# The feed-forward part of a Mamba block: channels on the partitions, ternary first weights, steps between the drain's slots

## The reference

```python
x = x + attn(layernorm(x))            # Mamba: 32 heads of 64, state 64, 8 groups
x = x + ffn(layernorm(x))

def layer_norm(x, g, b):              # biased variance, eps 1e-5
    return (x - mu) * rsqrt(var + eps) * g + b
def ternary_quant(w):
    scale = 1.0 / clip(mean(abs(w)), 1e-5)
    wq = clip(round(w * scale), -1.0, 1.0) / scale
    return w + stop_gradient(wq - w)  # in value: wq
def ffn(x):
    h = layer_norm(x, ln1_g, ln1_b)               # 128 features
    h = h @ ternary_quant(w1).T + b1              # to 512
    h = gelu(h, approximate=False)
    h = layer_norm(h, ln2_g, ln2_b)               # over 512
    return h @ ternary_quant(w2).T + b2           # to 128
```

## Time and profile before

| what | us |
|---|---|
| runs shown | 1182.76, 1175.94, 1181.65 (median 1181.65) |
| the profiled execution | 1176.72 |
| its span, first to last instruction | 1174.8 |
| busy in the span: PE, DVE, ACT, POOL | 1052.5 (90%), 1092.0 (93%), 969.3 (83%), 859.4 (73%) |

### The profile page before, as it was taken

The page is one execution under the profiler, slowest core; times in us unless marked ns, Lnnn a source line. Parts: engine busy times, 40 slices in busy tenths (PEclk is TensorE's granted clock), DMA queues, the critical chain, the costliest instruction groups (busy, mean ns, idle before and its releaser), DMA issues.

```text
span 1174.8 us, 26568 instructions
## 1 busy us (share of the span) xinstructions
PE 1052.5 (90%) x8966; PEld 734.7 (63%) x8966; DVE 1092.0 (93%) x2040; ACT 969.3 (83%) x2832; POOL 859.4 (73%) x596
## 2 busy tenths in 40 slices
PE   1724789999999999999999999999999999976886
PEld 1613566766766676776676667676666766643665
DVE  7597999999999999999999999999999999757985
ACT  2766989999999999999999999999999999823543
POOL 7300368888888888888888888888888888993331
PEclk9998999999999999999999999999999999989999
DMA  7310000000000000000000000000000000103001
GB/s 166 126 72 0 11 2 1 1 2 2 28 2 2 1 28 1 2 2 28 1 2 1 28 2 2 2 28 1 2 1 20 2 2 2 37 30 117 29 25 37
DMA packets 28756, 24.94 MB, mean 21 GB/s; under 512 B 12112, under 2 KB 22992, under 8 KB 28368
## 3 DMA queue, kind: packets, MB, share of 16 engines
q1 hardware_dynamic: 21584, 21.16, 5.9%
q10 hardware_dynamic: 7040, 2.12, 0.7%
HBM read 14.88 MB, written 8.39 MB: 20 GB/s over the span
## 4 chain that ended last, share of the span: by engine, by line
PE 73%; DVE 14%; issue 6%; POOL 3%; ACT 2%; ACTq 1%; POOLq 0%; DVEq 0%
PE bank L1596 10%; PE bank L1578 9%; PE bank L1610 8%; PE bank L1511 8%; PE bank L1527 8%; PE bank L1513 6%; PE bank L1512 6%; PE bank L1567 5%; PE bank L1548 5%; DVE conv L1127 4%; PE bank L1649 3%; PE bank L1621 2%; DVE lm L1117 2%; PE bank L1441 1%; PE bank L1662 1%
## 5 line engine op out<-in xcount | busy, mean ns | idle before, releaser
L1127 DVE SCALAR_TENSOR_TENSOR conv<-bank,cw,conv 128x509 f32<-128x509 f32 (+2 forms) x576 | 420.2, 740 | 16.0 <-ACT conv L725 8.6
L621 POOL TENSOR_TENSOR lm<-lm,cbs 128x1024 f32<-128x1024 f32 x128 | 304.1, 2376 | 69.3 <-ACT xw L820 69.3
L1117 DVE TENSOR_TENSOR_SCAN lm<-bank,ident 128x512 f32<-128x512 f32 x256 | 298.5, 1207 | 1.0 <-PE bank L1527 1.0
L865 ACT ACTIVATE xdt<-bank,dt_all 128x64 f32<-128x64 f32 x1024 | 221.5, 327 | 35.4 <-PE bank L1548 35.4
L820 ACT ACTIVATE xw<-xdt,lm 128x64 f32<-128x64 f32 x768 | 198.9, 363 | 0.0
L629 POOL TENSOR_TENSOR ssum<-ssum,sq 128x512 f32<-128x512 f32 x96 | 123.1, 1283 | 89.4 <-ACT sq L880 88.9
L1511 PE MATMUL bank<-xn_hi,w_hi 128*128 128x512 f32 x320 | 164.6, 514 | 15.1 <-DVE conv L1127 14.3
L602 POOL TENSOR_TENSOR gated<-gated,gate 128x512 f32<-128x512 f32 x128 | 164.6, 1286 | 15.0 <-DVE gated L1174 13.2
L611 POOL TENSOR_TENSOR gated<-gated,rbs 128x512 f32<-128x512 f32 x128 | 165.3, 1292 | 1.1 <-ACT rbs L949 1.1
L831 ACT ACTIVATE conv<-bank,cb_bias,cw 128x512 f32<-128x512 f32 x189 | 141.2, 779 | 11.0 <-PE bank L1513 6.5
L1596 PEld LDWEIGHTS bank<-lm,xdt 128*64 128x64 f32 x2048 | 109.9, 137 | 63.4 <-issue 63.4
(11 more groups left out here) (175 smaller groups left out, 1780.4 us busy)
## 6 DMA issues: line engine op xcount, KB each, us to landing
lm<-in_L_attn_in_proj_w SPq DMA_DIRECT2D x1, 2048.0 KB, 11.6
xn_scratch<-chan SPq DMA_DIRECT2D x4, 512.0 KB, 4.7
r_stage<-residual_scratch SPq DMA_DIRECT2D x8, 256.0 KB, 2.9
x_scratch<-r_stage SPq DMA_DIRECT2D x8, 256.0 KB, 2.0
cbs<-x_scratch SPq DMA_DIRECT2D x8, 256.0 KB, 2.9
gated<-x_scratch SPq DMA_DIRECT2D x1, 2048.0 KB, 7.9
out_tokens<-gated ACTq DMA_DIRECT2D x8, 256.0 KB, 2.3
xn_stage<-xn_scratch SPq DMA_DIRECT2D x7, 256.0 KB, 3.2
```

The source lines that it names most:

```text
L621: gp.tensor_tensor(lm[:, mr, :, :], lm[:, mr, :, :], cbs[:, :, :], ALU.mult).then_inc(m_done, 1)
L865: act.activation(xdt[:, r, at:at + HP], misc_of("xt", n)[:, at:at + HP], ACT.Copy, scale=dt_h).then_inc(xdt_done, 1)
L1117: V.tensor_tensor_scan(lm[:, m % R, a, :], bc_bank[(3 * m + a) % 2][:, :], ident4[:, :], 0.0, ALU.mult, ALU.add).then_inc(scanned, 1)
L1127: V.scalar_tensor_tensor(out=conv[:, ci % 4, shift:S], in0=tile_bank(b, n, t)[:, 0:S - shift], scalar=cw[:, q, t, KW - 1 - shift:KW - shif ...
```

## The change

`step(i)` is rewritten for all engines, and its channels now lie on the partitions throughout. The normalised rows (without scale) are transposed as before; ACT writes them times g1 as float32r (`high_rows`), DVE the rest (`low_rows`). w1 becomes a matrix of -1, 0 and 1 (`w1q`, float32r), so that the first product is two single-piece products of 512 columns for each of four tiles, into two banks in turn. Its scale and bias (b1 and the part that comes from b of the norm, `b1s`) are operands of the Gelu. The hidden layer norm is moved behind the second product: w2 times g2 is centred over its rows and scaled (`centre_second`), a column pair with 1/sqrt(512) gives the sums of the hidden channels (WCOL = 130 columns), ACT squares the hidden tiles, DVE and POOL add the four of them, PE sums them over partitions (`square_sums`), DVE forms the variance (`hidden_variance`), POOL the power (`hidden_root`), and DVE multiplies and adds onto the rows (`results`). b2 and the part of b of the norm become one row `bias2`, which POOL adds to the rows (`add_bias`).

The steps stand behind slots of the drain, by engine, and all quantising behind its slots 0 to 5. In the drain norm products of m >= LATE_M = 8 are made by DVE instead of POOL. Each batch's rows have a place of their own (`fx[i]`, in tensors as they fall free); batch 7's stay where they are made. SP stores the results. The loop over steps is written out. The core of the diff (removed `step` and `quantise` bodies stand in the listing above; other bodies are cut to their waits and work):

```diff
-SUM_SLOTS, QUANT_SLOTS, QUANT_END = (5, 6), (6, 7), 12
-EARLY_STEPS = {12: -2, 13: -1, 14: 0}
+LATE_M = SLOTS - 8
+PE_STEPS = {4: (0,), 6: (1,), 8: (2,), 10: (3,), 14: (4,), 15: (5, 6, 7, 8)}
+ACT_STEPS = {4: (0,), 7: (1,), 8: (2,), 13: (3,), 14: (4,), 15: (5, 6, 7)}
+DVE_STEPS = {4: (0,), 6: (1,), 8: (2,), 13: (3,), 14: (4,), 15: (5, 6, 7, 8, 9)}
+POOL_STEPS = {4: (0,), 7: (1,), 8: (2,), 13: (3,), 14: (4,), 15: (5, 6, 7, 8, 9)}
...
+            sp.wait_ge(cdec_done, NB * SLOTS - R)
+            sp.wait_ge(skipped, NB * SLOTS - 7)
+            load(0)
+            load(1)
...
+            sp.wait_ge(xdt_done, 2 * CH * NB * SLOTS)
+            load(2)
+            load(3)
             sp.wait_ge(m_done, NB * SLOTS)
+            load(4)
+            load(5)
...
+            for i in range(NB):
+                sp.wait_ge(f_out, CH * i + CH)
+                sp.dma_start(out[i].rearrange("(c p) d -> p c d", p=P), fx[i]).then_inc(f_stored, 16)
...
@@ gpsimd @@
                     bb, m = back(b, n, LAG_NORM)
+                    if b == NB and m >= LATE_M:
+                        return
...
+            def row_root(i):
+                gp.wait_ge(f_xaggr, CH * i + CH)
+                gp.tensor_tensor(ve_x, mv_x[:, :, 1], eps_c[:, 0:CH], ALU.add).then_inc(f_xeps, 1)
+                gp.tensor_tensor(r_x, ve_x, neghalf[:, 0:CH], ALU.pow).then_inc(f_xr, 1)
+            def hidden_root(i):
+                gp.wait_ge(f_y, 2 * i + 2)
+                gp.tensor_tensor(r_h, ve_h, neghalf[:, 0:CH], ALU.pow).then_inc(f_hr, 1)
+            def add_bias(i):
+                gp.wait_ge(q_bias2, 1)
+                gp.tensor_tensor(fx[i], fx[i], bias2..., ALU.add).then_inc(f_xb, 1)
+            def add_squares(i):
+                gp.wait_ge(f_add_v, i + 1)
+                for t in range(2, HT):
+                    gp.wait_ge(f_sq, HT * i + t + 1)
+                    gp.tensor_tensor(total, total, fsq[t][0], ALU.add).then_inc(f_add, 1)
+            def step(i):
+                hidden_root(i - 2)
+                add_bias(i - 1)
+                row_root(i + 2)
+                add_squares(i)
...
+                if n == 1:
+                    row_root(0)
+                if n == 3:
+                    row_root(1)
...
@@ scalar @@
+            def gelu(i, t):
+                act.wait_ge(f_mm1, HT * i + t + 1)
+                act.activation(fge[:, i % 2, t, :], h_bank[t % 2][:, :], ACT.Gelu, scale=qs[:, 12:13],
+                               bias=b1s[:, t:t + 1]).then_inc(f_gelu, 1)
+            def step(i):
+                gelu(i, 0)
+                gelu(i, 1)
+                high_rows(i + 1)
+                hidden_square(i, 0)
+                gelu(i, 2)
+                hidden_square(i, 1)
+                gelu(i, 3)
+                if i == 2:
+                    expand_root(NB, 9)
+                hidden_square(i, 2)
+                hidden_square(i, 3)
...
+                if n == 1:
+                    act.wait_ge(q_load, 32)
+                    for k in range(2):
+                        act.activation(qt[:, k, :], qw[:, k, :], ACT.Abs, accum_out=qs[:, k:k + 1]).then_inc(q_abs, 1)
+                if n == 3:
+                    act.wait_ge(q_t, 1)
+                    act.activation(w1q[:, :], bank[2][:, :], ACT.Copy).then_inc(q_copied, 1)
+                    high_rows(0)
+                    for k in range(2):
+                        act.wait_ge(q_rows, k + 1)
+                        act.activation(qw[:, 0, :], (qw[:, 1, :], qt[:, 1, :])[k], ACT.Copy, accum_out=qs[:, 16 + k:17 + k]).then_inc(q_acc, 1)
+                        act.wait_ge(q_acc, k + 1)
+                if n == 4:
+                    act.wait_ge(q_t, 2)
+                    act.activation(w2x[:, :, 0:DM], bank[3]..., ACT.Copy).then_inc(q_copied, 1)
...
@@ vector @@
+                if b == NB and n >= LATE_M + LAG_NORM - SLOTS and back(b, n, LAG_NORM) is not None:
+                    V.tensor_tensor(gated[:, v % 2, m % R, :], gated[:, v % 2, m % R, :], rbs[:, :], ALU.mult).then_inc(normed_v, 1)
...
+            def results(i):
+                dve.wait_ge(f_hr, i + 1)
+                dve.wait_ge(f_xb, i + 1)
+                for c in range(CH):
+                    V.scalar_tensor_tensor(out=fx[i][:, c, :], in0=result_bank..., scalar=r_h[:, c:c + 1],
+                                           in1=fx[i][:, c, :], op0=ALU.mult, op1=ALU.add).then_inc(f_out, 1)
+            def step(i):
+                hidden_variance(i - 2)
+                row_stats(i + 2)
+                results(i - 2)
+                low_rows(i + 1)
+                row_normalise(i + 2)
+                first_squares(i)
...
+            def ternary(k, done):
+                w, t = qw[:, k, :], qt[:, k, :]
+                qchain(V.tensor_scalar(t, w, q_scale[:, k:k + 1], 1.0, ALU.mult, ALU.min))
+                qchain(V.tensor_scalar(t, t, -1.0, MAGIC, ALU.max, ALU.add))
+                V.tensor_scalar(t, t, MAGIC, None, ALU.subtract).then_inc(done, 1)
+            def quantise_second():
+                ternary(1, q_two)
+                V.tensor_tensor(qw[:, 1, :], qt[:, 1, :], g2row, ALU.mult).then_inc(q_rows, 1)
+                V.tensor_tensor(qt[:, 1, :], qt[:, 1, :], b2beta, ALU.mult).then_inc(q_rows, 1)
...
+                if n == 1:
+                    row_stats(0)
+                if n == 2:
+                    row_normalise(0)
+                    quantise_first()
+                if n == 3:
+                    row_stats(1)
+                    quantise_second()
+                    low_rows(0)
+                    row_normalise(1)
+                    hidden_bias()
+                    centre_second()
...
@@ tensor @@
+            def first_product(i, t):
+                pe.wait_ge(f_lo, i + 1)
+                reach(pe, f_gelu, HT * i + t - 1)
+                MM(h_bank[t % 2][:, :], w, fhi[i % 2], start=True, stop=False)
+                MM(h_bank[t % 2][:, :], w, flo[i % 2], start=False, stop=True).then_inc(f_mm1, 1)
+            def second_product(i, c):
+                for t in range(HT):
+                    last = MM(result_bank(i, half)[:, at:at + WCOL], fge[:, i % 2, t, P * c:P * c + P], w2x[:, t, :],
+                              start=(t == 0), stop=(t == HT - 1))
+            def step(i):
+                first_product(i, 0)
+                first_product(i, 1)
+                row_transposes(i + 1)
+                second_product(i - 1, 0)
+                first_product(i, 2)
+                second_product(i - 1, 1)
+                first_product(i, 3)
+                second_product(i - 1, 2)
+                square_sums(i - 1)
+                second_product(i - 1, 3)
```

More of the change, by code:

```diff
@@ new lines, in row_stats @@
+            def row_stats(i):
+                if not item(i):
+                    return
+                if i < NB - 1:
+                    dve.wait_ge(f_loaded[i], 16)
+                else:
+                    dve.wait_ge(x1_done, NB)
+                reach(dve, f_xn, CH * i)
+                for c in range(CH + 1):
+                    if c > 0:
+                        dve.wait_ge(f_xstats, CH * i + c)
+                    if c < CH:
+                        V.bn_stats(bn_x[:, c, :], fx[i][:, c, :]).then_inc(f_xstats, 1)
+                    if c > 0:
+                        V.bn_aggr(mv_x[:, c - 1, :], bn_x[:, c - 1, :]).then_inc(f_xaggr, 1)
@@ new lines, in results, with first_squares @@
+            def results(i):
+                if not item(i):
+                    return
+                dve.wait_ge(f_hr, i + 1)
+                dve.wait_ge(f_xb, i + 1)
+                for c in range(CH):
+                    at = WCOL * (c % 2)
+                    V.scalar_tensor_tensor(out=fx[i][:, c, :], in0=result_bank(i, c // 2)[:, at:at + DM], scalar=r_h[:, c:c + 1],
+                                           in1=fx[i][:, c, :], op0=ALU.mult, op1=ALU.add).then_inc(f_out, 1)
+            def first_squares(i):
+                if not item(i):
+                    return
+                dve.wait_ge(f_sq, HT * i + 2)
+                V.tensor_tensor(fsq[0][i % 2], fsq[0][i % 2], fsq[1][0], ALU.add).then_inc(f_add_v, 1)
@@ L1409, in _ @@
-            for b in (NB - 1, NB):
-                for n in range(SLOTS):
-                    slot(b, n)
-                    if (b, n) == (NB, SUM_SLOTS[0]):
-                        V.memset(ones, 1.0).then_inc(q_ones, 1)
-                    if b == NB and n in QUANT_SLOTS:
-                        quantise(QUANT_SLOTS.index(n))
-                    early(step, b, n)
-            dve.wait_ge(xo_ready, NB)
-            ffn_steps(step, dve.Fori)
+            q_mean, q_scale, q_inv, q_neg, q_gain, q_sum = (qs[:, 4 + 4 * k:6 + 4 * k] for k in (0, 1, 2, 4, 5, 6))
@@ new lines, in _ @@
+            for n in range(SLOTS):
+                slot(NB - 1, n)
+            for n in range(SLOTS):
+                slot(NB, n)
+                if n == 0:
+                    V.memset(ones, 1.0).then_inc(q_ones, 1)
```

(17 more changed lines are left out.)

518 lines of the change are left out of this document (258 added, 260 removed).

## The result

The kernel after takes 1144.66 us (median of 4 runs, 1142.59 to 1147.83), the kernel before 1181.62 (1175.94 to 1182.76): a ratio of 0.97, 95% interval 0.9674 to 0.9726. The forecast was 1136 (1120 to 1156). Its profiled execution has a span of 1143.9 us, 14.1 above the forecast span of 1129.8.

The account below looks back on a forecast made before the run. POOL was taken to bound the drain and DVE the feed-forward part, 12.1 us a batch. Drain and step terms summed to span 1131.7 against 1176.7, a gain of 45.0; on the median's level 1136.7, forecast 1136, range 1120 to 1156.

Parts of the forecast that it names:

- PE's and the loop's terms: Late feed-forward steps: order bounds the loop, 8.2 us a batch instead of 12.1; PE (7.1) takes over in the last steps.
- row_normalise(0) 2.0 (beside POOL): Drain slot 2 on DVE: normalising the first batch's rows beside a working POOL would add 2.0 us.
- the decay product: POOL's last decay product, drain slot 4: forecast to start near 1042 us, waiting for ACT's weighing behind its copies with sums.
- (d): Drain: each of five steps costs its whole chain, 25 us with PE partly at half clock; slower, 125 giving 1221; chance 0.06.
- Step 0, slots 5 to 7, step 1: Drain followed on POOL: step 0 ends at 1052.9 us, slots 5 to 7 at 1062.9, step 1 at 1069.8.
- The end: After the last output's transpose near 1098: PE bounds steps 5 to 8, to 1123.7; variance, power, results, store to 1129.8.
- steps 2 to 4: Drain followed on POOL: step 2 takes 8.1 us, to 1080.4; step 3 ends at 1091.6, step 4 at 1099.7.
- slot 4: Drain on POOL: decay 2.35, norm 1.26, power 1.64; slot ends at 1047.2 us, where it ended at 1036.5.
- (a): Drain waits overlap better than the in-order reading: 1115 in span, 1122 on the median's level; decay product before 1037; chance 0.14.
- (b): DVE and POOL exclude each other, upper price everywhere in first slots and norm products: 14 us more, 1150; chance 0.16.
- (c): Square is not in Gelu's table set on ACT: loads of 1.28 alternate, 1182, no change; chance 0.03.
- (e): The change gives back one for one in stretch what the drain takes in: near 1180; chance 0.03.

Follow-up runs that it names:

- e3: Kernel after with row_root placed ahead of add_bias on POOL: median 1146.7 us.
- e6: Kernel after with add_bias moved from POOL to DVE, between low_rows and row_normalise: median 1144.8 us.
- e9: Kernel after with row_normalise(0) in two DVE instructions over 512 columns instead of four: median 1146.39 us.
- e7: Kernel after with the ternary passes and two quantising products on 8 of 512 columns: median 1141.66 us, ratio to before 0.9673.
- e5: Kernel after with eleven filler matmuls added on PE in slots 3 and 5 of the drain: median 1144.38 us.
- e1: Kernel after with all feed-forward steps behind slot 15, none between the drain's slots: median 1155.71 us, ratio to before 0.9794.
- e10: Kernel after with row_normalise(0) in two instructions, the tiny square reading PSUM, and filler matmuls in slots 3 and 5: median 1144.61 us.
- e12: Kernel after run once more, unchanged: median 1144.84 us.

## Why the prediction was right, and where its size was off

The direction and the mechanism held, and the time lay in the range, 8.7 us above the forecast. In the profiled execution part of that is luck: TensorE kept its clock behind the 1.87 us gap in step 3, where its fall cost five of the edited kernels 1.7 to 3.4 us.

- **PE's and the loop's terms.** Late periods of 8.5, then 6.2 us; forecast 8.2, then PE's 7.1 and less. That the order and not an engine is the bound was right, and it held to the end, where I had PE take over. e3 and e6 show how firmly: of 1.3 us taken from POOL's part of the loop, 0.3 or nothing is left, since DVE takes the rest. From the end of step 1 to that of step 4 it took 29.2 us, forecast 29.9.
- **The term that was mis-sized: "row_normalise(0) 2.0 (beside POOL)".** It measured 5.62. I had bounded the ternary passes from both sides by their prices beside and without POOL, but took the four instructions of row_normalise at some 0.5 each, not far above the 0.37 mean of a group that lay where POOL had little to do. The extra is not a share of the work but a wait for POOL's current instruction, paid again by each short instruction: (5.62 - 1.10) / 4 = 1.1 us each. This is 3.6 of the 4.0 us by which the decay product came later than forecast; e9, which has two instructions in place of four, took 1.6 us off both. I had cited the Trainium skill, "SBUF — State Buffer", section "SBUF: two separate sides", that the two engines exclude each other for whole instructions; the 8 columns of e7 that took 2.26 us agree (though not every GpSimd instruction holds DVE, as the last section shows), and I should have priced by instructions, not by bytes.
- **PE's clock, a term I left out of the forecast.** I had it only as part of rival (d). The gap of 7.90 us that the quantising opens put PE at half clock in slot 3; gaps of 2.69 us in step 0 and 3.87 in slot 6 did so again. Filling the first and the last (e5) gave 1.2 us ahead of the decay product and 1.6 more up to the end of step 1.
- **Step 0, slots 5 to 7, step 1**: 7.1, 12.1 and 8.1 us, forecast 5.7, 10.0 and 6.9, together 4.7 over my sums. The 1.6 of the clock is in it, and so are POOL's waits of 0.74, 1.60 and 0.74 us in the slots where I had 1.2 in all, and one more hold on the shared port, now on POOL's side, where step 1's sum lies beside two norm products of DVE. POOL in order of time, 2.25 instead of 1.26:

```profile
1079.49 2.25 POOL L704 TENSOR_TENSOR xdt<-xdt,chan 128x512 f32<-128x512 f32 x1 [1.83 <-DVE xdt L1447]
```

- **The end.** From the transposed last output to the end of the span 33.2 us, forecast 31.6. Here PE was not the bound, as I had it, but still the loop.
- The sum: 4.0 + 4.7 - 0.7 (steps 2 to 4) - 0.3 (slot 4, and the last output's place within step 4) + 1.6 = 9.3 us in the tail. With the 4.8 ahead of the mark, the 14.1 of the span.
- **Rivals.** (a) fell: the decay product was 35.5 us behind the mark, 26.6 or less was its sign. (b) was half right: the upper price is real and is paid at more places than I gave it, but in the eight norm products it came to little (0.85 on the mean against 0.7 free). (c) fell with one table load at Gelu's line. (d) fell, and e1 shows the interleaving to be a gain of 9.7 us, not a loss. (e) fell.

## What to carry to other kernels

Price DVE instructions that have all their operands in SBUF, beside a GpSimd busy with large products, by their count: each short one can wait out the GpSimd instruction in flight, so give it one long instruction, or an operand in PSUM, or a place where GpSimd stands. When work is moved into an earlier stage, ask which engine it leaves idle there: a gap on TensorE can be paid twice, by the gap and by the half clock behind it (here behind 7.90 and 3.87 us, and behind 1.87 us in some profiles). And in a loop bound by its order, taking work off one engine of the chain moved the wait to the next (e3, e6); the period fell, from 8.5 to 6.2 us, where two links of the chain, row_root and row_normalise, fell away.

## What the runs showed that I had not expected

- An element-wise DVE instruction on 128x8 lasted 2.26 us, as long as GpSimd's 128x1024 product beside it (2.35), against 0.17 alone. In the kernel after, one on 128x2 (L1509) took 2.31 us beside the same product.
- Not every GpSimd instruction holds DVE. In slot 3 of the kernel after, row_root's power (128x4) ran for 1.20 us, and two of DVE's instructions beside it took no more than their free price; the next one, beside a gate product (from 1046.15), took 1.65. GpSimd and DVE in order of time:

```profile
1044.97 1.20 POOL L677 TENSOR_TENSOR xn_stage<-xn_stage,neghalf 128x4 f32<-128x4 f32 x1
1045.33 0.43 DVE L1477 TENSOR_SCALAR conv<-conv 128x512 f32<-128x512 f32 x1
1045.79 0.69 DVE L1492 TENSOR_TENSOR conv<-conv,chan 128x512 f32<-128x512 f32 x1
```

- The same gap of 1.87 us on TensorE ahead of the same products let the granted clock fall in some profiles (to 0.50 in e10's window from 1098 to 1102) and not in others (1.00 in e12); the price was 1.7 to 3.4 us. Small gains ahead of that point were lost there; whether by chance or by something in the edits is open.
- Gelu, Square, Copy and a scaled Copy shared one table: one load of 1.28 us in the whole feed-forward part.
